# A second staging room per stream in the shifted cross attention, and new step tables for all engines

## The reference

```python
x = x + _L1_attn_ref(_layernorm(x, axis=-1), ...)
x = x + _L1_xattn_ref(_layernorm(x, axis=-1), ctx_1024, ctx_1024, mask_1xSxS2_bf1, ...)
x = x + _L1_ffn_ref(_layernorm(x, axis=-1), ...)
```

```python
qh = (q @ w_q).reshape(b, t, N_HEADS, D_K).transpose(0, 2, 1, 3)
pe = sinusoidal_pe(H_SIZE, 2 * s)[::-1].astype(q.dtype)
ph = (pe @ w_p).reshape(2 * s, N_HEADS, D_K).transpose(1, 0, 2)
ac = jnp.einsum('bhtd,bhsd->bhts', qh + b_u[None, :, None, :], kh)
bd = jnp.einsum('bhtd,hmd->bhtm', qh + b_v[None, :, None, :], ph)
bd = left_shift(bd)
scores = (ac + bd) / math.sqrt(D_K)
scores = jnp.where(mask[:, None, :, :], scores, jnp.float32(-jnp.inf))
attn = jax.nn.softmax(scores, axis=-1)
out = jnp.einsum('bhts,bhsd->bthd', attn, vh).reshape(b, t, H_SIZE)
return out @ w_o
```

## Time and profile before

| | |
|---|---|
| median of 3 runs | 2349.49 us (2343.83 to 2353.4) |
| profiled execution | 2348.47 us, its span 2346.5 us |
| mean granted clock of TensorE | 0.941 of full speed |
| TensorE, VectorE, ScalarE busy | 86%, 62%, 47% of the span |
| bytes moved by DMA | 155.57 MB |

### The profile page before, as it was taken

How to read it: one execution, slowest core, us unless ns; L and a number is a source line. 1 busy time by engine, 2 the same in 40 slices (tenths; PEclk the granted TensorE clock), 3 DMA queues, 4 the chain that set the end, 5 groups by cost and what they waited for, 6 DMA issues and landing times.

```text
span 2346.5 us, 41892 instructions
## 1 busy us (share of the span) xinstructions
PE 2016.8 (86%) x15996; PEld 1603.5 (68%) x15996; DVE 1449.7 (62%) x4778; ACT 1113.9 (47%) x2842; POOL 232.3 (10%) x194
## 2 busy tenths in 40 slices
PE   6688999999975686789996888899999977769999
PEld 5455776667753464458885776666999855658998
DVE  5588317778775675776766676664333475566554
ACT  2277336666645575572223554446544455422222
POOL 3300000000020000001011000000111253100000
PEclk9799999999996797899997999999999988889999
DMA  4333000000018678661004234220000023210000
GB/s 159 80 96 84 34 21 1 1 1 1 1 56 224 185 191 220 183 176 73 1 1 110 59 87 104 66 61 2 1 1 1 26 69 100 84 64 10 8 5 6
DMA packets 169312, 155.57 MB, mean 66 GB/s; under 512 B 10628, under 2 KB 157852, under 8 KB 168472
## 3 DMA queue, kind: packets, MB, share of 16 engines
q1 hardware_dynamic: 169112, 152.89, 23.6%
HBM read 89.06 MB, written 63.39 MB: 65 GB/s over the span
## 4 chain that ended last, share of the span: by engine, by line
PE 56%; DVE 20%; DMA 10%; ACT 6%; SPq 3%; issue 2%; POOL 2%; ACTq 0%; DVEq 0%
PE banks L604 51%; DMA stacks<-region 5%; ACT P L1294 3%; SPq L2305 3%; DMA skew<-region 2%; DVE region L1669 2%; DVE P L1606 2%; PE banks L917 2%; DVE P L1859 2%; DVE region L1606 1%; DVE P L1839 1%; DVE region L1909 1%; ACT region L1294 1%; POOL route L2274 1%; DVE P L1610 1%
## 5 line engine op out<-in xcount | busy, mean ns | idle before, releaser
L604 PE MATMUL banks<-xnT,region 128*128 128x256 f32 x1696 | 428.6, 385 | 14.6 <-ACT kz L1294 4.8
L604 PEld LDWEIGHTS banks<-xnT,region 128*128 128x128 f32 x1696 | 309.2, 192 | 57.6 <-ACT kz L1294 8.5
L1294 ACT ACTIVATE P<-P,negm 128x256 f32<-128x256 f32 x512 | 254.4, 501 | 101.2 <-DVE negm L1859 61.3
L604 PEld LDWEIGHTS banks<-region,kz 128*128 128x128 f32 x2304 | 277.2, 193 | 15.9 <-ACT kz L1294 4.5
L1294 ACT ACTIVATE kz<-banks,perm 128x256 f32<-128x256 f32 x400 | 168.2, 472 | 248.9 <-PE banks L604 247.0
L604 PE MATMUL banks<-region,kz 128*128 128x128 f32 x2304 | 280.8, 276 | 6.0 <-DVE x L1614 3.7
L1294 ACT ACTIVATE P<-banks 128x512 f32<-128x512 f32 (+2 forms) x392 | 185.8, 512 | 142.3 <-PE banks L604 139.0
L2185 POOL TENSOR_TENSOR rstd<-rstd,pows 128x2 f32<-128x2 f32 x96 | 69.4, 724 | 1680.7 <-DVE rstd L1610 1680.4
L1614 DVE SCALAR_TENSOR_TENSOR x<-banks,w,x 128x128 f32<-128x128 f32 x256 | 78.0, 347 | 194.3 <-PE banks L604 185.8
L1617 DVE TENSOR_REDUCE negm<-banks 128x2 f32<-128x512 f32 (+1 forms) x264 | 150.6, 592 | 56.1 <-PE banks L604 52.7
L604 PE MATMUL banks<-kz,qs 128*128 128x256 bf16 (+1 forms) x512 | 129.0, 284 | 28.9 <-DMA kz<-stacks 13.7
(11 more groups left out here) (243 smaller groups left out, 4002.1 us busy)
## 6 DMA issues: line engine op xcount, KB each, us to landing
stacks<-region SPq DMA_DIRECT2D x178, 192.0 KB, 3.0
skew<-region SPq DMA_DIRECT2D x64, 256.0 KB, 3.2
qs<-stacks SPq DMA_DIRECT2D x24, 408.0 KB
kz<-stacks SPq DMA_DIRECT2D x48, 192.0 KB
skew<-region SPq DMA_DIRECT2D x64, 128.0 KB, 2.8
skew_room<-skew SPq DMA_DIRECT2D x32, 256.0 KB, 3.5
P<-skew SPq DMA_DIRECT2D x32, 256.0 KB, 3.2
region<-stacks SPq DMA_DIRECT2D x34, 192.0 KB, 3.0
```

The lines of the kernel that those rows point to most:

```text
L604: return p.e.matmul(o, lhsT, rhs, start=start, stop=stop)
L1294: return a.e.activation(o, i, f, **kw)
```

## The change

There are two edits and new tables.

Each stream gets a second staging room, in places of region1 that held the weights of L0_attn and L0_xattn (stream 0) and the signs of L0_ffn (stream 1). Heads of even pairs use the first room, those of odd pairs the second. ScalarE's copy of head 2p waits for the transfer of pair p-2 and not of p-1. At its first two heads of the first batch ScalarE waits for the end of L0_ffn in both streams, since only then the places are free.

```diff
+    second_at = (0, after_early + 4 * TOK * S)
+    staging = [[staging[n], region1[:, second_at[n]:second_at[n] + 2 * TOK * S].rearrange("p (h t c) -> p h t c", h=2, t=TOK)] for n in range(2)]
...
-                    if h >= 2:
-                        pair = h // 2 - 1
+                    if h < 2 and j == 4 * ITEMS:
+                        yield
+                        for z in streams:
+                            a.wait_ge(z.x_done, 3 * ITEMS)
+                    if h >= 4:
+                        pair = h // 2 - 2
                         yield
                         a.wait_ge(s.skew_out[pair % 2], pairs_out[pair % 2] + 32 * (pair // 2 + 1))
-                    act(flat2(staging[s.n][:, h % 2, :, :])[:, 128:], s.S1[:, 128:]).then_inc(s.shift_out, 1)
+                    act(flat2(staging[s.n][h // 2 % 2][:, h % 2, :, :])[:, 128:], s.S1[:, 128:]).then_inc(s.shift_out, 1)
...
-                        dma(s.skew[slot, :, t * 128:(t + 1) * 128, far:S].rearrange("h p m -> p h m"), staging[s.n][:, :, t, far:],
+                        dma(s.skew[slot, :, t * 128:(t + 1) * 128, far:S].rearrange("h p m -> p h m"), staging[s.n][slot][:, :, t, far:],
```

All five strings of `TURNS` are new. They agree with the old ones up to L0_xattn and differ from there to the end of the program. The first line in which ScalarE's table differs, as an example of how they read:

```diff
-        "0270104601020062003700340039004300201063004020b3100310600123001701300109003202030033003310801003002010b3206100"
+        "0270104601020062003700340039004300201063004020b310031060012300170130010900320203003300331063004010430070100310"
```

More of the change, by code:

```diff
@@ L46 @@
[L46 to L50, removed]
@@ new lines @@
+        "23001300410033103200410030100200101031103400130013003001010023011301210111003600410032001100320041003200440034"
+        "00330012002300130051001300130041001300120041001200110025002100110012005200210021002200220021002100420013002100"
+        "32003100140011003100210013002200110041002100130022003100230013003200110011001200120011002100210021004400310022"
+        "00110012002300110024001400110031001100330033004100210013002200310023001300320011001100120012001100210021002100"
+        "44003100220011001200230011002400140011003100110033003300410021001300220031002300130032001100110012001200110021"
@@ new lines @@
+        "00210021004400310022001100120023001100240014001100310011003300330041002100130022003100230013003200110011001200"
+        "1200110021002100210034100320031007045300220046001100j300310044002600520012004400120024004200121032003200530022"
+        "001210020020100101230013123500100103003200520021004300170032001200420042004100d3005300320012007010140052001200"
+        "54002200121002002210240014103400130031030200330021014200250019003100560042004200420062003100g02010103300201001"
+        "00140044001400240016002400240019003301100103006201260020014500420011004300410026004200120052004200410022002100"
@@ new lines @@
+    "gpsimd": ("3l1100110011j0110011002200110011001100110011004200130011001100110022001100110011002200101012010101011022012010"
+        "01091090030031001100110011001100110011001101101001011010101001011050010522002200220022001100101001001001001001"
+        "0010010010010010010050010010050100110011"),
+    "sync": ("29110011j02100110034002200110033006600660b110022001020100220552244025102520032002300520035002300ah312021504142"
+        "0010012001250254025300a200af10031002100a00200150214041520055005001040150020102f010021002100k200a10201150029002"
+        "520235002400550055009s0050060011001100200140100301011042010310500105103100300105104100100101001410410010010100"
+        "131040080090440044004400448a0088008800880011001100110011"),
@@ L466, in program @@
                for n in range(2)]
+    second_at = (0, after_early + 4 * TOK * S)
+    staging = [[staging[n], region1[:, second_at[n]:second_at[n] + 2 * TOK * S].rearrange("p (h t c) -> p h t c", h=2, t=TOK)] for n in range(2)]
+    assert where[("early", "L1x_q")][0] >= 2 * TOK * S and second_at[1] + 2 * TOK * S <= at_ph
     at_second = at_staging + 4 * TOK * S
@@ L470, in program @@
     assert at_second + 2 * TOK * D <= 3 * E * F
-    q_rooms = [[s.wide[:, 0:2, :], staging[s.n][:, 0, :, :]] for s in streams]
-    k_rooms = [[s.wide[:, 2:4, :], staging[s.n][:, 1, :, :]] for s in streams]
+    q_rooms = [[s.wide[:, 0:2, :], staging[s.n][0][:, 0, :, :]] for s in streams]
+    k_rooms = [[s.wide[:, 2:4, :], staging[s.n][0][:, 1, :, :]] for s in streams]
     W2 = {n: cols(region2, "L1a", n) for (p, n) in where if p == "L1a"}
```

132 lines of the change are left out of this document (60 added, 72 removed).

## The result

| | before | after |
|---|---|---|
| median of 6 runs, us | 2351.18 (2343.83 to 2354.46) | 2333.51 (2327.89 to 2338.01) |
| ratio, 95% interval | 1 | 0.9928 [0.9908, 0.9948] |
| profiled execution, its span, us | 2346.5 | 2330.5 |

The changed kernel is 0.7% faster, some 17 us. I had predicted 2328 us, 21 less than before.

What follows compares the result with a forecast made beforehand. No engine is full overall; L1_xattn's four bubbles are held by DMA and the staging room. Profiled 2348.5 us, with -18 - 8 - 3 + 0 + 8 = -21 and +1 to the median, gives 2328 us; range 2295 to 2362 us.

Steps and rivals of the forecast that it cites:

- likeliest case: The prediction's own forecast for the whole kernel: 2312 to 2337 us, chance 0.45.
- A: L1_xattn's bubbles (batch changes): the second staging room shortens ScalarE's wait and so TensorE's; -18 us, ends 0 and -51.
- the smaller of stall and free time: Per L1_xattn bubble, the lesser of TensorE's stall and DMA's free time: 23.5 us together, three quarters taken.
- B: L1_xattn: streams some 10 us further apart, one's front transfers beside the other's dense work; -8 us, ends 0 and -20.
- C: SyncE's queue: stream 0's first query and key pieces move ahead, cutting TensorE's kz waits; -3 us, ends 0 and -7.
- First rival: L1_xattn: DMA binds already, the pairs queue on busy engines and waits move to VectorE; about 2352 us, chance 0.24.
- a bubble can't become shorter than its DMA work: L1_xattn's bubbles: bytes stay the same, so free DMA time caps each gain at 8.0, 4.8, 6.7 and 8.7 us.
- Second rival: L1_xattn: all was latency, so ScalarE's waiting for the room goes whole; about -54, 2295 us, chance 0.14.
- D: ScalarE's new wait at the first two heads, for the end of L0_ffn, is already met; 0 us.
- E: Program's end: less lag loses FFN cover (+22 at worst), earlier L3_attn and fronts apart gain; +8, ends -10 and +25.
- third rival: Program's end pays: both streams go through L3_xattn together with no FFN beside them; about 2366 us, chance 0.17.
- mirror image: L1_ffn to the second FFN: stream 1 leads by 0.4 batch where it trailed by 0.4; 0 us, wrong beyond 10.

Runs made afterwards that it cites:

- room_only: Second staging room and the distance of two pairs, with the old tables, against the kernel before; 2346.7 us, ratio 0.9981 to before.
- order_only: New tables with one staging room, without the wait for the end of L0_ffn, against the changed kernel; 2379.1 us, ratio 1.0114 to before.
- heavy_new: Changed kernel plus 64 extra transfers of 128 rows of 2 KB in L1_xattn (16.8 MB); 2364.6 us, ratio 1.0055 to before.
- light_new: Changed kernel plus 64 extra transfers of 128 rows of 16 bytes in L1_xattn; 2364.8 us, ratio 1.0056 to before.
- wide_new: Changed kernel with both transfers of a pair's way out at full width (8.4 MB more, as many issues); 2338.2 us, ratio 0.9945 to before.

## Why the prediction was right, and where it wasn't

The total was right (2333.5 in a range of 2295 to 2362, and in my likeliest case's 2312 to 2337), and the sign. The sum was -21, measured -17. That the sum came so near is luck: its parts miss by more than the total, and in both directions. By its own steps:

**A, the room, -18.** Half of the mechanism held: ScalarE's wait for it fell from 51.0 to 5.4 us (I had said below 15). But the step "the smaller of stall and free time" priced the room in the old order and in the bubbles. There it is worth 4 us (room_only), not 18, and the gaps don't shorten with it (111.4 and 110.8 us). Where it does pay, 42 us under the new order, it pays in the dense stretches, where I had given it nothing. What I left out is that a table of steps that was made for one room has the copies where one room allows them. Other waits of ScalarE and TensorE took the place at once.

**B, the streams further apart, -8, and C, kz earlier, -3.** B's effect on the bubbles is there and larger than I had it: the gaps lose some 36 us by the order alone, not 8 (no run tells the streams' distance from the rest of the tables). But the dense time gives it back, 65 us longer with one room and 24 with two. For C, TensorE's waits for kz rose from 11.8 to 32.6 us in place of falling. The new order isn't what makes them: order_only has 3.2, and room_only, with SyncE's old order, has 28.0. Both kernels with two rooms meet a kz wait of some 30 us, both with one room 3 to 12: it seems to have been hidden behind the wait for the room.

A, B and C together were -29. From L1_attn's end to L1_ffn's the measured difference is -10.5. This is the term that was mis-sized, by a factor of three: while ScalarE's wait for the room fell by 45.6 us, others grew (kz +20.8, VectorE for the shifted scores +26.8, ScalarE for negm +33.6 us). These three overlap, so they don't add, and that they are the same time which the room freed is argued from their sizes.

**First rival, DMA binds.** Its sign was there: VectorE's skew waits rose from 5.5 to 32.3 us, over the 20 I had named. But L1_xattn lasts 367 us and not 385, and heavy_new beside light_new shows that bytes aren't what binds. The share of 0.71 to 0.88 that I had set as a floor ("a bubble can't become shorter than its DMA work") was no floor that these runs bear out: 16.8 MB more than light_new raised the share over the block and neither the gaps nor the time. The packets do cost, in the dense time; by what way, the landing of the pairs or another, stays open.

**Second rival, all was latency.** Half true: it isn't bandwidth, but behind the first wait there were others.

**D, 0.** Nothing contradicts it: no wait of ScalarE for the end of L0_ffn stands out. It was not tried alone.

**E, the end of the program, +8 (ends -10 and +25).** From the end of L2_xattn on the difference is -4, and TensorE's idle time there 74.3 and 74.6 us, so about 0. The stretch from the second FFN's end until TensorE is full again shrank from 297 to 255 us, since the blocks are cut differently (the FFN ahead of it grew from 180 to 197), but its idle time is 69.5 and 70.6. Less lag between the streams cost no cover in sum. The third rival is out; whether the two effects of E cancel or neither is there, no run here separates. (Its price names "A to C at -8, as in the first rival", but the first rival has 0 to -5; with that the third would lie some 3 to 8 us higher.)

**What I took as 0.** L1_attn and what lies ahead of it became 8 us longer, which I had not looked at. The stages from L1_ffn's end to L2_xattn's end gave 9 us, which I had called a mirror image, with 10 us as the limit of being wrong. Both come with the new tables alone (order_only) and not with the room alone (room_only); which steps of the tables make them wasn't tried. So the total is right because errors cancel: 19 us too much for L1_xattn, 8 for the beginning, against 9 for layer 2 and 12 for the end.

A view that could have warned me stood in the trace of before: the other waits of the same engines. A wait is worth its length only up to the next one behind it, and in L1_xattn of the kernel before ScalarE stood 39.6 us for the maxima and 23.0 for TensorE beside the rows I read. These are the two that grew in room_only.

## What to carry to other kernels

A buffer more and an order of issue made for it are one change: here the buffer alone gained 4 us, the order alone lost 27, and both together gained 17, so a second buffer under an unchanged hand-made order says little about what it is worth. Before pricing a removed wait, list what else the same engines wait for in that stretch, since the next wait behind it sets the gain. Before calling a stretch DMA bound by its busy share, add bytes without packets and packets without bytes. And when two traces are compared by stretch, take stretches of equal length or of equal work: a bubble whose border has moved looks fuller than it is.

## What the runs showed of the hardware

64 transfers of 128 rows of 16 bytes cost as much as 64 of 128 rows of 2 KB (+30 us each), and 64 transfers of one row next to nothing (+3). The trace counts 144 packets for a transfer of 128 rows and 32 for one of a single row. Spread over the packets the price is 3.0 and 3.2 ns each in the new kernel and 4.2 in the old one (39 us over 9216). It is not the time for which the packets keep the DMA engines busy, which grew by 13 us in light_new and by 41 in heavy_new. The 16-byte rows may have a price of their own that happens to equal that of 2 KB; sizes between were not tried, but 8.4 MB more in as many packets (wide_new) showed 4 us, within the noise, which speaks against it. The added transfers themselves landed at 3.7 us in the median with 256 KB, at 4.0 with 2 KB in 128 rows and at 2.8 with 2 KB in one row. The Trainium skill ("DMA: Bandwidth & Descriptors", Anatomy of one DMA) reckons a transfer issued from GpSimd from its bytes and a fixed part; for these transfers, issued from SyncE, the measurement differs, as the bytes made no difference and the rows did. (The prediction took the two figures for SyncE's transfers without saying that they are given for GpSimd's.) About half of the price, by the estimate above, remains when the packets stand in another queue.
